# Four reorderings in the start-up of a pipelined two-layer attention kernel

## The reference, cut to what matters

```python
x = L0_attn_x                                    # (32, 256, 128)
xn = layernorm(x)
x = x + L0_attn(xn, ...) + L0_ffn(xn, weight, gamma, beta)
xn = layernorm(x)
x = x + L1_attn(xn, ...) + L1_ffn(xn, ...)
```

```python
gamma = max(abs(xn))          # over all 32 sequences, after the second norm
beta = mean(abs(weight))
w_q = clip(round(weight / (beta + 1e-5)), -1, 1)
```

## Time and profile before

| what | value |
|---|---|
| median of 3 runs | 2041.73 us (2040.42 to 2043.29) |
| profiled execution, its own time | 2045.01 us |
| its span | 2043.2 us, 48353 instructions |
| TensorE busy, products | 1863.3 us (91%) |
| VectorE busy | 1697.6 us (83%) |
| ScalarE busy | 1710.9 us (84%) |
| GpSimd busy | 1098.4 us (54%) |
| chain that ended last, by engine | PE 43%, DVE 36%, issue 14%, ACT 4% |
| mean of an exponential of 1024 elements (L1373) | 1024 ns |

### The profile page before, as it was taken

The page is one execution under the profiler, slowest core; times in us unless marked ns, Lnnn a source line. Parts: engine busy times, 40 slices in busy tenths (PEclk is TensorE's granted clock), DMA queues, the critical chain, the costliest instruction groups (busy, mean ns, idle before and its releaser), DMA issues.

```text
span 2043.2 us, 48353 instructions
## 1 busy us (share of the span) xinstructions
PE 1863.3 (91%) x16168; PEld 1505.2 (74%) x16290; DVE 1697.6 (83%) x3455; ACT 1710.9 (84%) x2256; POOL 1098.4 (54%) x1208
## 2 busy tenths in 40 slices
PE   3457999999999999999999999999999999999887
PEld 2245777777777777777877777777777777777776
DVE  6878889888888988888888888888988888898841
ACT  7336888888889888888988888888888888988887
POOL 5536555566655455665555566655556665544432
PEclk9688999999999999999999999999999999999998
DMA  6522332232233323322332232233323323332110
GB/s 156 148 66 63 87 89 76 61 88 78 58 84 85 87 58 77 88 64 68 85 88 67 67 88 66 66 86 87 77 58 88 80 59 81 85 88 63 28 45 6
DMA packets 302342, 155.16 MB, mean 76 GB/s; under 512 B 14388, under 2 KB 298324, under 8 KB 302292
## 3 DMA queue, kind: packets, MB, share of 16 engines
q1 hardware_dynamic: 302292, 154.52, 30.1%
HBM read 82.64 MB, written 71.30 MB: 75 GB/s over the span
## 4 chain that ended last, share of the span: by engine, by line
PE 43%; DVE 36%; issue 14%; ACT 4%; SPq 1%; DVEq 1%; POOL 1%; DMA 0%; POOLq 0%; ACTq 0%
PE pu L1771 8%; DVE zc L905 5%; DVE nmax L722 4%; PE pu L1581 3%; PE pav L1638 3%; PE pav L1581 2%; PE pm L1753 2%; PE pu L1601 2%; PE pav L1589 2%; PE pu L1615 2%; PE pm L1658 2%; DVE poly L874 1%; PE pav L1641 1%; PE pav L1761 1%; PE pu L1762 1%
## 5 line engine op out<-in xcount | busy, mean ns | idle before, releaser
L1202 POOL TENSOR_TENSOR zs<-zc,zs 128x1024 f32<-128x1024 f32 x192 | 450.7, 2361 | 132.5 <-ACT zc L1421 132.5
L1110 POOL TENSOR_TENSOR rs<-ve,mhalf 128x2 f32<-128x2 f32 x64 | 45.5, 711 | 415.7 <-DVE ve L690 412.5
L1771 PE MATMUL pu<-hid,h1t 128*128 128x256 f32 x1024 | 242.6, 380 | 0.0
L1771 PE MATMUL pu<-hid,h2t 128*128 128x256 f32 x1024 | 239.6, 382 | 0.0
L1420 ACT ACTIVATE zs<-zc,mhalf 128x1024 f32<-128x1024 f32 x192 | 218.5, 1138 | 0.4
L1421 ACT ACTIVATE zc<-zc,phalf 128x1024 f32<-128x1024 f32 x192 | 218.0, 1135 | 0.0
L1771 PEld LDWEIGHTS pu<-hid,h2t 128*128 128x128 f32 x1024 | 187.7, 191 | 24.9 <-ACT prob L1373 0.2
L1445 ACT ACTIVATE zs<-zs 128x1024 f32<-128x1024 f32 x192 | 201.4, 1049 | 2.0
L1771 PEld LDWEIGHTS pu<-hid,h1t 128*128 128x128 f32 x1024 | 185.6, 191 | 21.0
L1581 PE MATMUL pu<-k_st,q_st 128*128 128x256 bf16 (+1 forms) x1152 | 170.9, 254 | 30.3 <-DVE zc L905 16.7
L1439 ACT ACTIVATE zs<-zs 128x1024 f32<-128x1024 f32 x192 | 197.4, 1044 | 0.0
(11 more groups left out here) (285 smaller groups left out, 5262.2 us busy)
## 6 DMA issues: line engine op xcount, KB each, us to landing
scr<-parts SPq DMA_DIRECT2D x256, 192.0 KB, 2.4
q_st<-scr SPq DMA_DIRECT2D x128, 256.0 KB, 3.9
scr<-parts SPq DMA_DIRECT2D x128, 128.0 KB, 2.4
k_st<-scr SPq DMA_DIRECT2D x64, 256.0 KB
k_st<-scr SPq DMA_DIRECT2D x32, 512.0 KB, 5.1
x<-in_L_attn_x SPq DMA_DIRECT2D x32, 128.0 KB, 3.3
out<-xold SPq DMA_DIRECT2D x32, 128.0 KB, 1.8
q_st<-m_t SPq DMA_DIRECT2D x128, 4.0 KB
```

Of the source, the lines that this page charges most:

```text
L1202: G.tensor_tensor(zs[:, c], zc[:, c], zs[:, c], ALU.add).then_inc(sum_done.sem, 1)
L1771: last = PE.matmul(u.ap[:, c * T:(c + 1) * T], w[:, k, c * P:(c + 1) * P], src[:, k, :], start=(k == 0), stop=(k == HC - 1))
```

## The change

Four places are reordered. No instruction is added or removed.

1. Iteration 1, VectorE: `deep_weights` stands ahead of `values0` instead of behind it.
2. Opening, VectorE: the moments of sequence 1 stand ahead of the six maxima instead of behind them.
3. Opening, GpSimd: `residual0` stands ahead of the powers of the last chunk.
4. Opening, ScalarE: the last chunk is normalised ahead of the copy of the maxima.

```diff
@@ VectorE, iteration @@
                 if m:
                     normed1(run, m)
+                if run.quantise:
+                    deep_weights()
                 if f:
                     values0(run, f)
-                if run.quantise:
-                    deep_weights()
@@ VectorE, opening @@
                 latent_maxima(run, link)
+                dve.wait_ge(x_in.sem, x_in.at(a))
+                moments(st, mv, ve, x, LN_EPS, var0, of_norm(run))
                 for n in range(UNITS):
                     heads_reduced(unit(run, f"max{n}"), n, nblocks, ALU.max, True).then_inc(unit(run, f"max{n}").free, 1)
-                dve.wait_ge(x_in.sem, x_in.at(a))
-                moments(st, mv, ve, x, LN_EPS, var0, of_norm(run))
                 shift_lo(run, "mT", 0, f)
@@ GpSimd, opening @@
-                for c in range(PRE_CHUNKS):
+                for c in range(PRE_CHUNKS - 1):
                     chunk_scales(c)
                 pool.wait_ge(first_in, 16 * len(first))
                 residual0(run, f)
+                chunk_scales(PRE_CHUNKS - 1)
                 power(rs, ve, var0, rstd0, a)
@@ ScalarE, opening @@
                 chunk_normed(2)
+                chunk_normed(3)
                 shift_part(run, "mT", 0)
-                chunk_normed(3)
```

## The result

| | before | changed |
|---|---|---|
| median | 2041.69 us (12 runs, 2039.74 to 2043.29) | 2045.70 us (12 runs, 2043.08 to 2048.50) |
| profiled execution, own time | 2045.01 us | 2047.32 us |
| its span | 2043.2 us | 2045.6 us |

The ratio is 1.0021 (95%: 1.0012 to 1.0030): the changed kernel is 4.0 us slower. In a second comparison, beside later runs, it was 1.0017 (1.0008 to 1.0025), 3.5 us. The forecast was 2047.1 with a range from 2042.0 to 2050.5, most of the chance on slower.

The account below looks back on a forecast made before the run. The prediction took VectorE's in-order work in the opening to bound the kernel, not TensorE's 15.9 us wait. Its terms, -0.25 + 3.3 + 0.7 + 1.65 = +5.4 us on 2041.7, gave 2047.1 us, range 2042.0 to 2050.5.

Parts of the forecast that it names:

- VectorE has no hole: Opening: VectorE, executing in order, is busy during TensorE's 15.9 us wait for xf and leaves only 1.93 us to win.
- L: Opening, VectorE: delay of the extremes by GpSimd's mask selects now falling among them; 3.3 us, bounds 0 to 4.2.
- the deep weights: Iteration 1: values0 behind three products drains v's bank later, delaying qkv1a and VectorE's v_new; +1.65 us, bounds 0.8 to 1.9.
- the head: Opening up to the transposes of the extremes: -0.25 us without the masks' delay, plus 3.3 us for that delay.
- The clock: TensorE behind prob_l: after idling it runs at 1.2 GHz, so prob_l to the extremes' transposes takes 6.9 us, before 5.06.
- c: TensorE, extremes' transposes and attends: cost if the clock is still at 1.2 GHz there; 0.7 us, bounds 0 to 2.7.
- attends slow too: TensorE's attends: rival that they run at the low clock too; +7.4 us, 2049.1, chance 0.2.
- The sum: Whole kernel: -0.25 + 3.3 + 0.7 + 1.65 = +5.4 us, so 2047.1 us.
- the forecast's own case: Whole kernel: masks' delay of 2.5 to 4.2 us, low clock up to exp3, deep weights +1.65; 2045.6 to 2048.5, chance 0.38.
- The moments cost nothing: Opening, VectorE: moments of 1.1 us ahead of the maxima fit into its 2.07 us wait for TensorE; cost nothing.

Follow-up runs that it names:

- the moves alone: The changed kernel with the deep weights put back behind values0, so only the three reorderings of the opening: 1.0012 of the kernel before, 2.5 us more.
- the moments alone: The kernel before with only the moments of sequence 1 put ahead of the maxima: 1.0011 of the kernel before, 2.4 us more.
- the deep weights alone: The kernel before with only the deep weights put ahead of values0 in iteration 1: 1.0006 of the kernel before, 1.15 us more.
- the last experiment: The kernel before with only the four extremes of chunk 1 taken ahead of the latent maxima: 0.9987 of the kernel before, 2.8 us faster.

## Why the prediction was right, and where it was off

**VectorE has no hole.** Right: 15.9 us of TensorE's wait were removed, 13.1 came back, and the end followed VectorE. This step kept ten microseconds of gain out of the forecast. The sign then hung on L and the deep weights: with the masks held back, the head gained 0.60.

**L.** Predicted 3.3 within 0 to 4.2; measured 3.0 in all five profiles with this opening and free masks (the changed kernel twice, the moves alone, both runs with unread products), 2.9 with the moments alone and -0.1 with the masks held back. By a pair of extremes with 512-element selects beside it, 0.75 us are lost in 3.14, so some 0.38 a select, and the remaining 0.8 of 3.03 falls to the one of 1024. The scaling from the one operation that was held 0.92 us was near for that one; 0.54 for each of the six was too much, and so was the thought that it reaches the upper end. The rule of the Trainium skill (SBUF — State Buffer, "Who interferes with whom") names the pair of engines and the kinds of operands rightly, and by it L is nothing without the masks, which the trace shows. Summed with the full length of each select, 4.9, it would have been 1.9 too high: where both engines have queued work, each is stretched by a part, here VectorE's pair from 2.39 to 3.14 us and the select from 0.64 to 1.61.

**The clock.** Predicted 6.9 us from prob_l's end to the transposes; measured 6.62 and 6.61 (5.06 before), and 6.08 in the three moves alone, where the clock rose before the end. The estimate of half speed for each product was right for the changed kernel, the overlaps somewhat better. Head in all, from m_t to the transposes: before 26.94, changed 29.49 in both profiles, +2.55. Predicted was +3.05 with the 0.15 by which m_t was to come sooner, so +3.20 from m_t on. The difference of 0.65 is 0.27 of L, 0.28 of the clock and 0.10 that prob_l gained by following the folding without a gap.

**c.** Predicted 0.7 within 0 to 2.7. Measured 0 in one profile of the changed kernel, 2.3 less 0.7 in the other, and 1.2 in the three moves alone: both ends were met, by chance of the execution. Two kernels with the old order of the moments (the deep weights alone and the last experiment) also had part of their attends at the low clock, the second o_t ending 5.2 us behind the transposes' start instead of 4.1. The rival "attends slow too" is thus not another cause but an execution that occurs. The 0.7 given back at L815 was not foreseen.

**The deep weights.** The mechanism was right: the bank of v gates qkv1a, and the hole was 1.80 us. The term was mis-sized: 1.89 on the spot, 0.24 over the 1.65 predicted, since the product took 1.62 and not 1.46 and there are hand-overs of 0.15 before it. Its median alone was only 1.15 us above before, with an interval from -0.6 to 3.1. The prediction carried all of it to the end; a part may have come back in iteration 2, and that stays open, as said above.

**The sum.** Predicted was +5.4; the medians say +4.0 and +3.5. On the spot the traces show 2.4 (head, with m_t's 0.16) + 0 to 1.6 (attends) + 1.89 (deep weights) = 4.3 to 5.9, and with the deep weights' median of 1.15 in place of the 1.89 it is 3.5 to 5.1. So the mechanism was right and the size too high: L by 0.3 and the clock by 0.3, and c was 0 in one of two profiles. Whether a part of what is lost on the spot comes back later is argued, not shown, since the interval of the first comparison, 2.4 to 6.1 us, holds both sums. That the measured 2045.70 fell into the forecast's own case (2045.6 to 2048.5) was luck: it is 0.1 us inside, and the second comparison's 3.5 us would have been outside.

**Small ones.** exp1 came at 56.28, not 58.3: the rows of m_t landed some 1.2 us after the last issue ended (55.12), and the 3.0 us that x takes to land were no measure for four transfers of 4 KB. It made no difference, since TensorE only waited longer. x was issued at 38.14, 1.16 sooner: 0.67 of it is the shift of SP's queue, and the 0.49 left is what the residual's move gave (up to 0.6 predicted). The 0.15 us by which m_t should come sooner did come: it began 2.26 us after the start of the last maximum before (2.24 in the deep weights alone) and 2.10 in the changed kernel, in both profiles, and in the moments alone. The moments cost nothing, as said. The residual beside VectorE's extreme stretched that from 1.19 to 1.62 us and this stayed hidden in the wait that follows, as said.

**What is not settled.** Why the clock differs between executions of one order, in the attends and elsewhere. What the low clock costs in the whole time: up to the extremes' transposes the traces show 1.6 us (6.62 against 5.06 before) to 2.2 (against 4.4 behind the 108 products), but no run raised the clock and left everything else alone. And whether the deep weights cost the whole time their full 1.89 us.

## What to carry to other kernels

A long wait of one engine is worth what the next engine in the chain leaves open: look first at whether the engine that makes its next input has a hole, here 1.93 us against 15.9. Work that is freed early starts to run beside other work, so ask for each instruction of it whose operands it will meet; here seven selects, which had cost nothing behind the extremes, cost 3.0 us among them. What paid was the other way round: empty the binding engine first (1.3 parts in a thousand alone), then reorder behind it, and hold back what collides (3.1 in all; that each step adds to the one before is what the medians say, and their intervals overlap).

## What the runs showed of the hardware

A GpSimd select of 512 elements a partition beside back-to-back VectorE operations with two SBUF inputs takes 1.61 us instead of 0.64 and costs VectorE 0.38; one of 1024, 2.07 instead of 1.09, and about 0.8. GpSimd loses more than it takes. So did its chain for xf in the kernel before: the last step took 4.29 us instead of 1.19, while the twelve extremes beside it needed 14.48 us from the first start to the folding, and 14.37 with the masks held back, when GpSimd was idle.

TensorE's clock rose to 1.00 (2.4 GHz) between 62 and 63 in the kernel with 76 unread products and between 67 and 68 in that with 108, although both do the same up to 63.5 and beyond. And with 76 products it stood at 1.00 until about 76.2 and then fell to 0.50 (1.2 GHz): the engine had stood still from 71.99 to 75.53 and had been at work again for 0.7 us when it fell.
